# State products of 64 rows: two tiles on the two halves of the array, in a state-space block with a Fourier layer

## The reference

```python
xn    = (x - mean) / sqrt(var + 1e-5) * ln_gamma + ln_beta
delta = sigmoid(xn @ w_delta + b_delta)            # 16 states
B_t   = xn @ w_in + b_in
gate  = sigmoid(xn @ w_gate + b_gate)              # 512 columns
h     = tanh(h_previous * delta @ A + B_t)         # a scan over the 2048 rows
y     = (h @ C) * gate                             # 16 states -> 512 columns
x1    = layernorm(x + (y + x))
f     = real(ifft(fft(x1) @ (w_freq_real + i*w_freq_imag))) + bias
out   = layernorm(x1 + f)
```

## Time and profile before

| | |
|---|---|
| median of 3 runs | 938.47 us (938.18 to 939.08) |
| profiled execution, its own time | 938.36 us |
| span of the profiled execution | 936.6 us |
| busy share of PE, DVE, ACT, POOL | 97%, 80%, 59%, 46% |
| second pass, 545 to 900 us | PE busy in all of it |
| state products of 128 rows (L1321) | 120, one a tile from tile 8 on |

### The profile page before, as it was taken

One profiled execution on the slowest core, in us unless ns is written; L12 is line 12 of the kernel. 1 busy time (PEld: TensorE's weight loads), 2 busy tenths in 40 slices (PEclk: granted clock), 3 DMA queues, 4 the chain that ended last, 5 costly groups with the idle time before them and its releaser, 6 DMA issues.

```text
span 936.6 us, 19186 instructions
## 1 busy us (share of the span) xinstructions
PE 912.6 (97%) x5748; PEld 517.0 (55%) x5748; DVE 749.0 (80%) x1501; ACT 554.1 (59%) x1047; POOL 430.9 (46%) x865
## 2 busy tenths in 40 slices
PE   6999999999999999999997999999999999999997
PEld 3555555555555555555875555555555555555553
DVE  6988878888887878889567888888888888888883
ACT  2533333333333333335464588888888888888887
POOL 1432222222222222224124677777777777777772
PEclk9999999999999999999999999999999999999999
DMA  9434554455444554452604466776667766677653
GB/s 330 142 127 144 179 179 135 141 173 179 148 142 158 179 166 139 143 179 91 225 1 96 167 229 227 265 253 231 236 230 260 262 228 229 241 249 265 228 180 135
DMA packets 89482, 175.84 MB, mean 188 GB/s; under 512 B 3057, under 2 KB 5361, under 8 KB 89458
## 3 DMA queue, kind: packets, MB, share of 16 engines
q1 hardware_dynamic: 89024, 175.00, 54.9%
q10 hardware_dynamic: 434, 0.54, 0.3%
HBM read 106.45 MB, written 67.11 MB: 185 GB/s over the span
## 4 chain that ended last, share of the span: by engine, by line
PE 91%; DVE 4%; ACT 1%; issue 1%; POOL 0%; DVEq 0%; POOLq 0%
PE bank L1168 23%; PE bank L1169 23%; PE bank L1171 23%; PE bank L1158 12%; PE bank L1321 3%; PE bank L1213 2%; PE bank L1192 1%; PE bank L1195 1%; PE bank L1272 1%; PE bank L1265 1%; DVE h_lo L1039 1%; DVE gsum_sb L915 0%; DVE bn L895 0%; PE bank L1312 0%; PE bank L1229 0%
## 5 line engine op out<-in xcount | busy, mean ns | idle before, releaser
L907 DVE SCALAR_TENSOR_TENSOR lo_sb<-bank,hi_sb 128x512 f16<-128x512 f32 x256 | 176.7, 690 | 141.6 <-ACT hi_sb L578 76.5
L441 ACT ACTIVATE hi_sb<-bank 128x512 f16<-128x512 f32 x128 | 76.4, 597 | 264.1 <-PE bank L1158 264.1
L676 POOL TENSOR_TENSOR x_sb<-x_sb,gate_sb 128x512 f32<-128x512 f32 x128 | 164.0, 1282 | 75.0 <-DMA x_sb<-x 58.2
L1168 PE MATMUL bank<-wg_hi,hi_sb 128*128 128x512 f16 x512 | 194.0, 379 | 1.7 <-DVE gsum_sb L915 0.8
L1169 PE MATMUL bank<-z_sb,hi_sb 128*128 128x512 f16 x512 | 194.0, 379 | 0.0
L1168 PE MATMUL bank<-z_sb,hi_sb 128*128 128x512 f16 x512 | 194.0, 379 | 0.0
L1169 PE MATMUL bank<-wg_lo,hi_sb 128*128 128x512 f16 x512 | 194.0, 379 | 0.0
L632 POOL TENSOR_TENSOR veps<-mv,c_eps 128x1 f32<-128x1 f32 x128 | 24.2, 189 | 315.4 <-DVE mv L888 315.4
L1158 PE MATMUL bank<-cst,norm_sb 128*128 128x128 f32 x1024 | 159.4, 279 | 10.0 <-DVE norm_sb L901 8.2
L1158 PEld LDWEIGHTS bank<-cst,norm_sb 128*128 128x128 f32 x1024 | 118.4, 142 | 36.5 <-issue 8.9
L1171 PE MATMUL bank<-z_sb,lo_sb 128*128 128x512 f16 x512 | 131.4, 379 | 0.0
(11 more groups left out here) (161 smaller groups left out, 1225.9 us busy)
## 6 DMA issues: line engine op xcount, KB each, us to landing
x_sb<-x SPq DMA_DIRECT2D x63, 1024.0 KB, 6.3
gate_dram<-gate_sb SPq DMA_DIRECT2D x32, 1024.0 KB, 5.2
gate_sb<-gate_dram SPq DMA_DIRECT2D x32, 1024.0 KB, 5.6
out<-out_sb SPq DMA_DIRECT2D x31, 1024.0 KB, 5.3
h_rep<-fourier_constants SPq DMA_DIRECT2D x2, 514.0 KB, 13.0
x_sb<-x SPq DMA_DIRECT2D x2, 512.0 KB, 6.5
w_ring<-w_gate SPq DMA_DIRECT2D x2, 512.0 KB, 6.4
w_re_sb<-w_freq_real SPq DMA_DIRECT2D x1, 1024.0 KB, 12.3
```

The source lines that it names most:

```text
L676: pool.tensor_tensor(x_sb[:, k // 4, k % 4], x_sb[:, k // 4, k % 4], gate_sb[:, k // 4, k % 4], ALU.add).then_inc(s_v, 1)
L907: nc.vector.scalar_tensor_tensor(lo_sb[:, k % 2].rearrange("p t r -> p (t r)"), ps_t[k % 2][:], ROW_SCALE, hi_sb[:, k % 2].rearrange("p t ...
L1168: nc.tensor.matmul(dst, hi_sb[:, k % 2, t], w_hi[:, t], start=(t == 0), stop=False)
```

## The change

The state products of tiles n+6 and n+7 are now issued together, in even slots. Each takes 64 rows instead of 128: tile n+6 the partitions 0 to 63, tile n+7 the partitions 64 to 127, into the two banks of `ps_y`. For that `h_rep` has another layout: on partitions 0 to 63 the high, high, low, low parts of the even batch of a pair (16 rows each), on 64 to 127 those of the odd batch. `c_parts` is one matrix instead of two. The copies into `h_rep` are 32 of 16 partitions instead of 16 of 32. The products read their states from `h_now`, a buffer of four slices at a fixed address; SP loads half of it from `h_rep` for every half octet, ahead of the gate.

```diff
-        c_parts = sb("c_parts", [P, 2, D], F16)
+        c_parts = sb("c_parts", [P, D], F16)
+        h_now = sb("h_now", [P, BATCH // 2, P], F16)
+        s_hnow = [sem(f"b_states_loaded{i}") for i in range(2)]
             def second_pass(v, q):
                 sp.wait_ge(s_v, v * 8 + 4 * q + 4)
+                if isinstance(v, int):
+                    for r in (2 * q, 2 * q + 1):
+                        sp.wait_ge(s_hrep[r], 8 * 16)
+                sp.dma_start(h_now[:, 2 * q:2 * q + 2],
+                             h_rep[:, 2 * q:2 * q + 2, bass.ts(v + 1, P)]).then_inc(s_hnow[q], 16)
                 load_gate(v + 1, q)
...
             def replicate_states(done):
-                for r in range(BATCH // 2):
+                for b in range(BATCH):
                     for seg in range(4):
                         src = (h_hi, h_hi, h_lo, h_lo)[seg]
-                        sp.dma_start(h_rep[32 * seg:32 * seg + 32, r, P:SEQ],
-                                     src[32 * r:32 * r + 32, P:SEQ]).then_inc(done[r], 16)
+                        row = P // 2 * (b % 2) + STATE * seg
+                        sp.dma_start(h_rep[row:row + STATE, b // 2, P:SEQ],
+                                     src[STATE * b:STATE * b + STATE, P:SEQ]).then_inc(done[b // 2], 16)
...
-            def c_parts_of(j, low):
+            def c_parts_of(low):
...
-                if k in (2, 4, 6, 8):
-                    c_parts_of((k - 2) // 4, (k // 2 + 1) % 2)
+                if k in (2, 4):
+                    c_parts_of((k - 2) // 2)
...
-            def states_out(n, k, v):
-                if isinstance(n, int) and n < 16 and n % 2 == 0:
-                    pe.wait_ge(s_hrep[k // 2], 4 * 16)
-                if before(n, 2):
-                    pe.wait_ge(s_gy, n - 1)
-                nc.tensor.matmul(ps_y[k % 2][:], h_rep[:, k // 2, bass.ts(v, P)], c_parts[:, k % 2],
-                                 start=True, stop=True).then_inc(s_y, 1)
+            def pair_states_out(n, k, v):
+                if k % 4 == 0:
+                    pe.wait_ge(s_hnow[k // 4], v * 16)
+                pe.wait_ge(s_gy, n)
+                for j in range(2):
+                    rows = slice(P // 2 * j, P // 2 * j + P // 2)
+                    nc.tensor.matmul(ps_y[j][:], h_now[rows, k // 2], c_parts[rows],
+                                     start=True, stop=True).then_inc(s_y, 1)
...
-                elif exists(n + 7):
-                    states_out(n + 7, (k + 7) % 8, v if k < 1 else v + 1)
+                elif k % 2 == 0 and exists(n + 6):
+                    pair_states_out(n + 6, (k + 6) % 8, v if k < 2 else v + 1)
...
-    for j in range(2):
-        for low in range(2):
-            c[:, C_PARTS + 2 * j + low] = (row // STATE % 2 == j) & (row // 32 % 2 == low)
+    for low in range(2):
+        c[:, C_PARTS + low] = row // STATE % 2 == low
```

More of the change, by code:

```diff
@@ L35 @@
 C_PARTS = 2 * P
-C_WIDTH = C_PARTS + 4
+C_WIDTH = C_PARTS + 2
 W_GAMMA, W_BETA, W_BIAS = 0, KT, 2 * KT
@@ L399, in _ @@
                 for r in range(BATCH // 2):
-                    sp.wait_ge(s_hrep[r], 4 * 16)
+                    sp.wait_ge(s_hrep[r], 8 * 16)
                 sp.wait_ge(s_final, 1)
                 replicate_states(s_hrep2)
+                for r in range(BATCH // 2):
+                    sp.wait_ge(s_hrep2[r], 8 * 16)
             second_pass(0, 0)
@@ L551, in _ @@
                 for r in range(BATCH // 2):
-                    act.wait_ge(s_hrep[r], 4 * 16)
+                    act.wait_ge(s_hrep[r], 8 * 16)
                 with act.Fori(2, LANES) as r:
@@ L806, in split_c @@
                 nc.vector.sem_inc(s_c_split, 1)
-            def c_parts_of(j, low):
-                column = C_PARTS + 2 * j + low
-                mask = cst[:, column:column + 1]
+            def c_parts_of(low):
+                mask = cst[:, C_PARTS + low:C_PARTS + low + 1]
                 if not low:
-                    wait_own(nc.vector.tensor_scalar(c_parts[:, j], c_hi[:], mask, None, ALU.mult))
+                    wait_own(nc.vector.tensor_scalar(c_parts[:], c_hi[:], mask, None, ALU.mult))
                 else:
-                    nc.vector.scalar_tensor_tensor(c_parts[:, j], c_lo[:], mask, c_parts[:, j], ALU.mult,
-                                                   ALU.add)
+                    wait_own(nc.vector.scalar_tensor_tensor(c_parts[:], c_lo[:], mask, c_parts[:], ALU.mult,
+                                                            ALU.add))
             def largest_bias():
@@ L1057, in _ @@
                 for r in range(BATCH // 2):
-                    dve.wait_ge(s_hrep[r], 4 * 16)
+                    dve.wait_ge(s_hrep[r], 8 * 16)
                 dve.wait_ge(s_seen, 1)
@@ L1299, in _ @@
                 for r in range(BATCH // 2):
-                    pe.wait_ge(s_hrep2[r], 4 * 16)
+                    pe.wait_ge(s_hrep2[r], 8 * 16)
             pe.wait_ge(s_split, 1)
```

## The result

The changed kernel takes 946.87 us (median of 4 runs, 943.74 to 947.56), the kernel before 938.78 us beside it (4 runs, 938.18 to 940.14). The ratio is 1.0078, with a 95% interval of 1.0052 to 1.0103. It is slower, by 8.1 us; 950.7 us were predicted, with 937 to 963. The profiled execution of the changed kernel is its fastest run, 943.74 us with a span of 941.9 us: 5.3 us over the 936.6 us of before. The trace shows where these 5.3 us lie; the median has 3 us more, which no trace shows, since both profiled executions of the changed kernel are of its shortest runs.

A forecast was written before the change was run, and what follows sets the result against it. PE's own instructions were taken to bound the second pass. From the profiled 938.36 us, +11.6 for the pairs, +1.0 for the start and -0.3 for the scan gave 950.7 us, range 937 to 963.

The forecast's parts named there:

- the pair: Second pass, 60 pairs of 64-row state products: 0.626 us each instead of 0.432, +11.6 us in all.
- the round trip: PE's switch from whole-array products to part-array ones and back, priced from one-row products: 0.36 us per pair.
- four parts: The switch's price on PE: in, 0.09 us gap and 0.11 open load; out, 0.09 gap and 0.07 longer transposes.
- The part for the open load: Weight load left unhidden at PE's switch: claimed about unchanged for the pair, as its float16 loads take 0.10 us each.
- The stagger: In each pair on PE, the second product starts 0.05 us after the first, halfway between 0 and 0.10.
- The case of a cheap switch: Rival for the pairs on PE: switching in and back costs 0.16 to 0.24 us, 938 to 944 us; chance 0.10.
- The start: Start of the second pass, once: 32 copies delay `h_now` and the gate; +1.0 us, with 0 and +4 as ends.
- the slow case: Start of second pass: half-size copies still take 0.63 us each, ending at 520.3 to about 521; PE waits up to 1.5.
- two slots ahead: Start of second pass: DVE waits 3.1 us for the gate, of which PE, running two slots ahead, sees little.
- The loads of `h_now`: Second-pass loop, 30 transfers of 64 KB: cost nothing while they land in less than 10 us.
- Off the path: Second-pass loop: POOL already waits for x, up to 2.2 us, without delaying the end.
- The scan: Two DVE operations on `c_parts` go, at steps 6 and 8: 0 to -0.5 us, taken as -0.3.

The follow-up runs named there:

- Experiment 4: Changed kernel with both products of a pair on rows 0 to 63, so they can't run at once: 955.6 us, ratio 1.0176.
- experiment 3: Changed kernel with both products taking all 128 rows from `h_now`, `c_parts` again two masked matrices with two more scan operations: 944.63 us, ratio 1.0067.
- experiment 5: Changed kernel with four state products issued behind one switch in every fourth slot, into four banks: 945.95 us, ratio 1.0077.
- Experiment 2: Kernel before, with only its 16 copies of 32 rows into `h_rep` made as 32 copies of 16 rows: 942.91 us, ratio 1.0034.
- experiment 9: Changed kernel without on-chip copies: states stored to DRAM by 8 stores, `h_now` loaded from there, the gate ahead of it: 937.86 us, ratio 0.9996.
- 1: Changed kernel, with octet 1's first half of `h_now` and gate loaded after four batches' copies, the other four batches' copies following: 944.19 us, ratio 1.0045.
- 6: Changed kernel with the states copied by way of DRAM, two stores and eight loads into `h_rep` instead of 32 copies: 944.56 us, ratio 1.0060.
- experiment 11: The changed kernel once more, as it is: 945.47 us, ratio 1.0071; its profiled execution took 943.74 us.
- Experiment 8: Changed kernel without the loads of `h_now` in the loop, the buffer being filled for octet 1 alone: 945.08 us, ratio 1.0061.
- 7: Changed kernel with states copied through DRAM (two stores, eight loads into `h_rep`) and four state products behind one switch: 943.44 us, ratio 1.0050.
- 10: Changed kernel with states stored to DRAM by 8 stores, `h_now` loaded from there behind the gate, and four products behind one switch: 936.30 us, ratio 0.9977.

## Why the prediction was right, and where it was not

The time (946.87 for 950.7) and the side were right. The working was not: of the 12.3 us that the sum gave, 11.6 were for the pair, and the pair costs nothing. Two small terms that were put near zero make the loss that the trace shows. That the time came out inside the range is luck: a term of 11.6 us that was nothing was made up for by some 5 us more at the start and in the loop, and by 3 us of the median that stay unexplained.

**The pair, +11.6 us forecast, 0 measured.** The step that failed is the price of the round trip, 0.36 us, taken over from the products of one row. It is 0.21 us for float16 products of 64 rows: 0.10 in and 0.10 to 0.11 out. In the forecast's own four parts, the two gaps of 0.09 us stayed, and the two loads in the open went from 0.11 and 0.07 to 0.01 us each. Experiment 4 shows this part by part: the second product starts 0.226 us after the first, one stream and 0.01, and the next full one 0.308 us after that, one stream and 0.09. The 0.36 came from products of one row, in float32 and two passes, with a float32 load behind them. In the trace of before a float32 load takes 0.14 to 0.18 us and a float16 one 0.10, which fits; but what made the switch dearer there, no run tells apart. "The part for the open load stays about as it is" was wrong: the forecast put 0.11 us of load on top of the gap of 0.09, and in the changed kernel the whole way in is 0.10. The stagger of 0.05 us was not there either. That is 0.626 - 0.43 = 0.20 us a pair, 12 us in all. What held is the form of the argument: one stream shared, plus a round trip, against two streams. Experiment 4 shows the shared stream, experiment 3 that the sum is zero. The case of a cheap switch, with 0.16 to 0.24 us and 938 to 944 us, describes the pair; it had a chance of 0.10. The rows showed four switches, all at products of one row in float32, and that this differs from the pair was named only as a point for the rivals.

The Trainium skill's rule that a switch of tiling mode has the engine drain (TensorEngine Tiling (Array Packing), Key Properties) agrees with the trace: 0.17 and 0.23 us of idle load side around the pair. Its 4 ns between the starts in different row groups (TensorE: Matmul & The Clock Gate, Part 3) agree too: both products of a pair share one row of 0.39 us, where one product alone has 0.38. And its speedup of up to 2 is the stream's: 0.216 us for two products. With the round trip a pair is at 1.0, and the four of experiment 5 at 0.86 / 0.65 = 1.3.

**The start, +1.0 us forecast with +4 as its end, +5.07 measured.** The issue times were right to a microsecond: the copies end at 520.58 (520.3 to 521 was the slow case), and `h_now` is issued at 522.02 (521.5). Half the rows don't halve the 0.63 us that a copy takes in the queue. `h_now` cost PE 1.7 us (up to 1.5 was forecast). The failed step is the sentence that PE, two slots ahead, sees little of DVE's wait. PE is two slots ahead only in the bank of the state products. Its Fourier products write a bank that DVE's `w_ring` frees, and `w_ring` stands behind the waiting operation in DVE's order, so 3.15 of DVE's 5.3 us came through. The rest is the landing: 6.46 us for the gate where 5.6 was taken, with x, the gate and `h_now` of two halves all issued within 3 us. Experiment 2 shows most of the start's loss with the copies alone, experiment 9 that all of it goes when the queue is free of them; 1 and 6 show how it moves to another transfer or another wait if the queue is not really emptied.

**The loads of `h_now`, 0 forecast, +0.8 us measured (+0.5 in the profile of experiment 11).** They landed early enough (3.6 us by the DMA issues of the loop), but x lands later there, 6.5 us in the median instead of 6.0. POOL's wait for x rose from 52.8 to 63.3 us and came through to PE in a few slots of 3.5 to 3.7 us, so the chain did not stay PE's alone, as the forecast had it. "Off the path" had a margin that was not worked out. Experiment 8 puts 1.0 us on them.

**The scan, -0.3 forecast, -0.40 measured:** inside its bounds. The operation at step 8 was the cause of the long `hd`: experiment 3 has both back.

**The 3 us between the profiled execution and the median.** The changed kernel's nine runs are three of 943.7 to 943.9 us with a mean granted clock of 0.996 or 0.997, and six of 945.5 to 947.6 us with 0.990 to 0.995. The kernel before has its runs at 0.997 within 937.9 to 938.9 us, and those at 0.993 at 939.9 to 940.1; but its runs at 0.994 lie from 937.6 to 939.0, so the clock alone does not order them. In the profiles of experiments 2, 4, 5, 6 and 8 a stretch at half the clock begins in a wait of the start or within 1.6 us behind it. Those of 1, 3 and 7 and both of the changed kernel have the wait and no such stretch; those of the kernel before, 9 and 10 have neither. That a wait at the start makes such a stretch likelier would fit: experiment 2's costs 1.6 us, so two of them would, as an estimate, be the 3 us. But both profiles of the changed kernel are of runs at 0.997, so it is not shown and stays open.

## What to carry to other kernels

A switch of the array's form has a price per group, not per product. Measure it with products of the kind that will run: here 0.21 us against a stream of 0.216 us, so two products behind one switch break even and four gain, on TensorE's side. Before crediting a saving on the bounding engine, work out the margin of the next wait in line; here a quarter to a third of it arrived at the end (1.6 us against the pair in the same queue, 2.2 against the kernel before, of some 6).

Copies that one queue issues take their time by their number, and what stands behind them is late by the sum. Look at every transfer and every wait behind them, not the next alone, and at the order of the engine that will wait: an operation behind the late one may free what the bounding engine needs next.

## What was not expected of the hardware

A copy of 16 partitions inside the chip took SP's queue 0.61 to 0.63 us, as one of 32 did, while a load of 1 MB from DRAM mostly took 0.37 to 0.51, and 0.94 at most. Of the eight stores of the states to DRAM in experiment 9, six took 0.6 to 0.8 us of the queue and two 2.5 and 2.6, all eight together 9.2 us, against 21 us for the 32 copies. Two products in different halves start together to within the 0.01 us that the rows resolve.
